# A hybrid block on one core: the first norm taken tile by tile, and the ternary quantiser's pieces moved within the gated steps

## The chip, the cores and the metric

One core of one Trainium2 chip runs one launch. The metric is the device time of that core in microseconds (us); the kernel before takes 2132.3 us (median of three runs, 2129.67 to 2132.58).

## The reference, cut to what matters

x is 2 x 1024 tokens of 512 columns. Four layers are added to it in turn, each on a layernorm of x: a gated linear recurrence ("gated attention"), a feed-forward layer with ternary weights, differential attention, and the same feed-forward layer again. The change lies in the first layer and in the work on the feed-forward weights that is done beside it:

```
proj = layernorm(x) @ w_in.T;  q, k, v, a, g = split(proj, 5)       # 16 heads of 32
q = q * rsqrt(mean(q*q) + eps);  k = tanh(k);  a = clip(sigmoid(a + 2), 0.6, 0.9995)
prefix = cumprod(a) in chunks of 64;  memory = the scan  m = a*m + k*v  over the tokens
y = sigmoid(g) * (q * memory) + (1 - sigmoid(g)) * v;  x = x + y @ w_out.T
# each group of 64 weights of w_gate_up (4096 x 512) and w_proj (512 x 2048):
scale = clip(mean(|w|), 1e-8);  w = scale * clip(round(w / scale), -1, 1)
```

## The kernel before, in words

The kernel has two phases; the change touches only `phase_first` (L265), which holds the gated layer and the first feed-forward layer. The 2048 tokens are four blocks of 512, and a block is four tiles of 128 tokens. The gated layer is 16 **gated steps**, s = 0 to 15; step s works on block s // 4 and on 128 of the 512 output columns (s % 4). The order of work is written out by hand for each engine, and the engines wait for one another on counting semaphores.

In a step TensorE (loop at L467) makes five projections of 128 columns by 512 tokens (`project`, L412, matmuls of L435), in the order q, k, v, a, g. Between them it puts in three one-matmul group sums for the quantiser (`group`, L440, matmul L444), the sums of squares of q (L453) and their spreading by transposes (L460). The three group sums stand after q, after v and after g. I call them **A, B and C** here: A after the first projection of a step, B after the third, C at the end.

The quantiser turns 48 pieces of 128 x 512 weights into ternary form, three in each step. ScalarE makes |w| and sign (`piece`, L538) and issues the load of the piece after next. TensorE's group sum adds |w| over 64 rows. VectorE's `quantise` (L722) reads that sum: L727 writes the scale and increments `scaled`, L730 compares |w| with it and increments `hits`. `hits` releases GpSimd (L647 to L664), which does four bf16 `tensor_tensor` operations on the piece in a row, each waiting for the one before. The group sum of the next piece waits for `scaled` (L443), because it writes the bank that L727 reads.

VectorE's step (L754) is: `finish` of the step before (L738, L740, L743, L749: four operations that end in yT), in some steps the rows of a norm, the first piece, mean and reciprocal for q (L764, L768), the product k*v (L774), the second piece, then a wait for the sigmoid of a (and, where a norm is turned, for its four transposed tiles), the clip (L787, L788), the first scan (L791), L793, the product with q that increments `q_scaled` (L796), the second scan (L798), a copy (L800), the third piece (L807), and in some steps the statistics of a norm. The steps are:

- `STATS_IN`: the statistics of a norm (`normal_stats`, L683: L691, L694, L696) at the end of steps 0, 1, 4, 5, 8, 12.
- `TURN_IN`: two steps later, in steps 2, 3, 6, 7, 10 and 14, the rows of that norm (`normal_rows`, L701: the reciprocal L705, then four `tensor_scalar` operations L708, one for each tile, issued with no wait between them). TensorE transposes rows 0 and 1 after B (`turn`, L388, transposes L397), rows 2 and 3 after the spreading; ScalarE copies each out of PSUM (`keep`, L552). The two PSUM banks are used in turn: tile 2 waits until tile 0 has been taken, tile 3 until tile 1 has. In steps 2, 3 and 7 the norm is of the kind "in" and `keep` frees the bank; in steps 6, 10 and 14 it is of the kind "mid" and VectorE's `keep_low` (L711, L715), which follows ScalarE's copy, frees it.
- `OUT_IN`: in steps 4, 8 and 12 the output projection of a block (L408).

ScalarE's step (L565) has after the copy of v: a wait for VectorE's reciprocal of q (L768), its square root (L586), which releases the spreading; a table load (L589); the two `keep` copies of a turned norm (L555); the sigmoid of a (L594); the third piece.

Before step 0 stands the norm of block 0: VectorE waits for the four tiles of x as they land, does the four statistics, then one variance operation (L696); ScalarE one square root (L550); VectorE the four rows (L708); TensorE transposes (L397), ScalarE copies (L555), and the first projection starts when the fourth copy is done. ScalarE issues the loads of the first two weight pieces (L558, L559) ahead of all that.

Of the kernel before, what the change touches and what calls it, by code (L numbers as in the profile page):

```python
# [9 lines left out]
ALU = mybir.AluOpType  # L10
# [10 lines left out]
TPB = BLK // P  # L21
# [13 lines left out]
class Steps:  # L35
# [5 lines left out]
    def did(self, ins):  # L41
        ins.then_inc(self.sem, 1)
        self.k += 1
        return ins
# [4 lines left out]
    def settle(self):  # L49

        self.eng.wait_ge(self.sem, self.value())
# [5 lines left out]
NP = 3  # L57
# [207 lines left out]
def phase_first(nc, core, x_in, w_inT, w_outT, w_guT, w_pT, wq1, wq2, wk):  # L265

    with ExitStack() as ctx:  # L267
# [41 lines left out]
        vec, gp = sem("s_vec"), sem("s_gp")  # L309
        bank, x = core["banks"], core["x"]  # L310
        W, h16 = core["W"], core["hT16"]
        w_stored = sem("w_stored")
        block = ctx.enter_context(nc.Block())

        def ring(s, j):
# [26 lines left out]
        def x_tile(blk, t):  # L342
            return x[:, (blk * TPB + t) * D:(blk * TPB + t + 1) * D]
# [184 lines left out]
        def _(act):  # L528
            def load(n):
                s, j = divmod(n, NP)  # L530
                i, c = divmod(s, KT)
                if j < 2:
                    src = w_guT[i * P:(i + 1) * P, (2 * c + j) * D:(2 * c + j + 1) * D]
                else:
                    src = w_pT[(i * KT + c) * P:(i * KT + c + 1) * P, :]
                act.dma_start(stage[n % 2], src).then_inc(piece_loaded[n % 2], 16)
# [9 lines left out]
                    load(n + 2)  # L546

            def root(g):
                act.wait_ge(var_ready, g + 1)
                act.activation(dev[g % 2][:, :], var[g % 2][:, :], ACT.Sqrt).then_inc(root_ready, 1)  # L550

            def keep(g, t):  # L552
                kind, blk = of(g)
                act.wait_ge(turned, g * TPB + t + 1)
                act.activation(half(blk, 0, t) if kind == "mid" else whole(blk, t), turn_bank(g, t),  # L555
                               ACT.Copy).then_inc(kept, 1)

            load(0)  # L558
            load(1)  # L559
            root(0)  # L560
            act.preload_act_table_set("sigmoid_and_others")
            for t in range(TPB):
                keep(0, t)
            act.wait_ge(const_ready, 1)
            for s in range(NSTEP):  # L565
                piece(NP * s)
# [100 lines left out]
        def _(dve):  # L667
# [15 lines left out]
            def normal_stats(g):  # L683
                kind, blk = of(g)
                b = g % 2
                for t in range(TPB):
                    if g == 0:
                        dve.wait_ge(first_loaded[t], 16)
                    elif kind == "in" and t == 0:
                        dve.wait_ge(x_loaded[blk], 16)  # L690
                    did(dve.bn_stats(stats[b][:, 6 * t:6 * t + 6], x_tile(blk, t)))  # L691
                settle()
                for t in range(TPB):
                    did(dve.bn_aggr(mv[b][:, 2 * t:2 * t + 2], stats[b][:, 6 * t:6 * t + 6]))  # L694
                settle()
                did(dve.tensor_scalar(var[b][:, :], mv[b][:, 1:2 * TPB:2], LN_EPS,  # L696
                                      1.0 / (UP * UP) if kind == "mid" else 1.0, ALU.add, ALU.mult))
                settle()
                dve.sem_inc(var_ready, 1)

            def normal_rows(g):  # L701
                _, blk = of(g)
                b = g % 2
                dve.wait_ge(root_ready, g + 1)
                did(dve.reciprocal(inv[b][:, :], dev[b][:, :]))  # L705
                settle()
                for t in range(TPB):
                    dve.tensor_scalar(row_of(g, t), x_tile(blk, t), mv[b][:, 2 * t:2 * t + 1], inv[b][:, t:t + 1],  # L708
                                      ALU.subtract, ALU.mult).then_inc(rows_ready, 1)
# [39 lines left out]
                dve.tensor_tensor(yT[:, c * BLK:(c + 1) * BLK], t1[:, :], vc, ALU.add).then_inc(y_ready, 1)  # L749
                dve.wait_ge(y_ready, s + 1)  # L750

            normal_stats(0)
            normal_rows(0)
            for s in range(NSTEP):  # L754
                i, c = divmod(s, KT)
                if s:
                    finish(s - 1)
                g = TURN_IN.get(s)
                if g is not None:
                    normal_rows(g)  # L760
                quantise(NP * s)

                dve.wait_ge(sq_summed, s + 1)
                did(dve.tensor_scalar(mean[:, :], bank[4][:, 0:HPQ], 1.0 / HD, RMS_EPS, ALU.mult, ALU.add))  # L764
                settle()
                if s:
                    dve.wait_ge(spread_root, s)
                dve.reciprocal(inv_q[:, :], mean[:, :]).then_inc(inv_ready, 1)  # L768
                if g is not None:
                    dve.wait_ge(turned, g * TPB + 1)  # L770

                dve.wait_ge(tanhed, s + 1)
                dve.wait_ge(v_kept, s + 1)
                did(dve.scalar_tensor_tensor(t1[:, :], ring(s, 1), 1.0 / FLOOR, v_sb[s % 2], ALU.mult, ALU.mult))  # L774
                settle()
                dve.sem_inc(dve_took, 1)
                quantise(NP * s + 1)
                if s in OUT_IN:
                    for t in (0, 1):
                        add_out(OUT_IN[s], t)  # L780
                if g is not None:
                    for t in (0, 1):
                        keep_low(g, t)
                    dve.wait_ge(turned, g * TPB + TPB)

                dve.wait_ge(sigmoided, s + 1)
                did(dve.tensor_scalar(a_first[:, 0:BLK:CH], ring(s, 3)[:, 0:BLK:CH], 0.6, 0.9995, ALU.max, ALU.min))  # L787
                did(dve.tensor_scalar(a_sb[:, :], ring(s, 3), 0.6, 0.9995, ALU.max, ALU.min))  # L788
                settle()
                dve.sem_inc(dve_took, 1)  # L790
                did(dve.tensor_tensor_scan(prefix[:, :], a_sb[:, :], a_first[:, :], 0.0, ALU.mult, ALU.max))  # L791
                settle()
                did(dve.scalar_tensor_tensor(t1[:, :], prefix[:, :], FLOOR, t1[:, :], ALU.min, ALU.mult))  # L793
                settle()
                dve.wait_ge(spread_done, s + 1)
                dve.tensor_tensor(prefix[:, :], bank[4], q_sb[:, :], ALU.mult).then_inc(q_scaled, 1)  # L796
                start = carry[:, c:c + 1] if i % (NBLK // NB) else 0.0
                did(dve.tensor_tensor_scan(t2[:, :], a_sb[:, :], t1[:, :], start, ALU.mult, ALU.add))  # L798
                settle()
                did(dve.tensor_copy(carry[:, c:c + 1], t2[:, BLK - 1:BLK]))  # L800
                if s in OUT_IN:
                    for t in (2, 3):
                        add_out(OUT_IN[s], t)
                if g is not None:
                    for t in (2, 3):
                        keep_low(g, t)
                quantise(NP * s + 2)  # L807
                if s in STATS_IN:
                    normal_stats(STATS_IN[s])
            finish(NSTEP - 1)  # L810

# [1023 lines left out]
```

## Time and profile before

| what | value |
|---|---|
| median of three runs | 2132.3 us |
| the profiled execution, its own time | 2131.86 us |
| its span, first to last instruction | 2130.0 us |
| PE, DVE, ACT, POOL busy | 96%, 60%, 40%, 42% of the span |
| mean granted TensorE clock, in parts of full speed | 0.989 |
| the 16 gated steps | 14.7 to 398.8 us of the span |

PE is TensorE's matrix unit, DVE is VectorE, ACT is ScalarE, POOL is GpSimd. In a timeline a row gives the start in the span, the duration, the engine, line, operation, what it writes and reads, how many operations were merged (x2), and in brackets how long the engine had been idle before it and what released it.

### The profile page before, as it was taken

The numbers are of one execution on the slowest core, as the hardware profiler recorded it, in microseconds if no ns is written. First come the engines' busy times: TensorE is split into PE (matmuls) and PEld (weight loads), VectorE is DVE, ScalarE is ACT, GpSimd is POOL, SyncE is SP. The second block draws the span as 40 slices with busy tenths as digits, with TensorE's granted clock in tenths as the row PEclk, the third lists the DMA queues.
The fourth block names the chain that finished last, engine by engine and source line by source line (L and its number), as shares of the span: only waits on it lengthen the run. The fifth ranks groups of instructions, "written<-read, shape, count | busy, mean of one in ns | idle before, by whom it ended". The sixth has DMA issues, their size and how long they took to land.

```text
span 2130.0 us, 29410 instructions
## 1 busy us (share of the span) xinstructions
PE 2035.2 (96%) x11824; PEld 902.1 (42%) x11824; DVE 1271.8 (60%) x1838; ACT 855.3 (40%) x1304; POOL 888.4 (42%) x457
## 2 busy tenths in 40 slices
PE   7998999999999999999999999999999879899999
PEld 3444444444444445343434334343433323444444
DVE  5868687647746634455555555555556623775634
ACT  4434353334434322434443434344344442443431
POOL 3766585600000001666666666766766681000000
PEclk9999999999999999999999999999999999999999
DMA  7111110300000011000001010000000101000001
GB/s 232 35 30 35 30 36 30 129 15 1 1 1 1 1 48 26 1 16 14 18 11 21 5 27 1 16 16 16 2 11 6 61 30 40 1 1 20 21 1 40
DMA packets 68999, 55.53 MB, mean 26 GB/s; under 512 B 36800, under 2 KB 55232, under 8 KB 68608
## 3 DMA queue, kind: packets, MB, share of 16 engines
q1 hardware_dynamic: 61952, 41.07, 6.6%
q10 hardware_dynamic: 6912, 12.59, 2.0%
q8 instruction: 94, 1.54, 0.3%
q14 instruction: 41, 0.34, 0.1%
HBM read 43.02 MB, written 10.62 MB: 25 GB/s over the span
## 4 chain that ended last, share of the span: by engine, by line
PE 53%; DVE 4%; ACT 3%; POOL 3%; issue 1%; DVEq 0%; ACTq 0%; POOLq 0%
PE psum L116 9%; PE psum L1151 8%; PE psum L1239 8%; PE psum L1300 6%; PE psum L1283 5%; PE psum L140 5%; PE psum L1189 3%; POOL b_totals L1524 2%; PE psum L1279 2%; PE psum L1245 2%; PE psum L1257 2%; DVE b_maxima L1587 2%; PE psum L1270 1%; PE psum L1197 1%; ACT b_probs L1446 1%
## 5 line engine op out<-in xcount | busy, mean ns | idle before, releaser
L1524 POOL TENSOR_TENSOR b_totals<-b_totals,b_probs 128x2048 f32<-128x2048 f32 (+3 forms) x160 | 515.4, 3221 | 311.1 <-ACT b_probs L1446 304.9
L1587 DVE TENSOR_REDUCE b_maxima<-psum 128x2 f32<-128x1024 f32 (+3 forms) x384 | 350.6, 954 | 392.4 <-PE psum L1245 232.9
L1446 ACT ACTIVATE b_probs<-psum 128x1024 f32<-128x1024 f32 (+3 forms) x320 | 228.6, 765 | 256.4 <-PE psum L1283 233.1
L435 PE MATMUL psum<-hT,a_win 128*128 128x512 f32 x640 | 293.1, 601 | 0.8 <-ACT hT L555 0.8
L116 PE MATMUL psum<-hT,b_early 128*128 128x512 f16 x1024 | 228.2, 383 | 5.2 <-DVE b_middle L202 5.2
L116 PE MATMUL psum<-hT,W 128*128 128x512 f16 x1024 | 226.4, 381 | 3.9 <-DVE a_win L202 3.9
L435 PEld LDWEIGHTS psum<-hT,a_win 128*128 128x128 f32 x640 | 120.4, 193 | 130.8 <-issue 129.5
L116 PEld LDWEIGHTS psum<-hT,b_early 128*128 128x128 bf16 x1024 | 100.2, 98 | 131.5 <-issue 10.6
L116 PEld LDWEIGHTS psum<-hT,W 128*128 128x128 bf16 x1024 | 100.4, 98 | 126.5 <-DVE a_win L202 7.6
L1501 POOL MEMSET b_mask<- 128x128 f32 x1 | 0.2, 204 | 356.8 <-POOLq L267 356.8
L1634 DVE RECIPROCAL b_down<-b_down 128x128 f32<-128x128 f32 x128 | 111.9, 918 | 40.7 <-ACT b_down L1424 40.7
L654 POOL TENSOR_TENSOR a_parts<-a_parts 128x512 bf16<-128x512 bf16 x48 | 60.0, 1251 | 135.2 <-DVE a_parts L730 135.2
L1239 PE MATMUL psum<-b_early 32*128 32x512 f32 (+3 forms) x768 | 106.8, 537 | 6.7 <-ACT b_probs L1446 3.1
L1239 PE MATMUL psum<-b_middle 32*128 32x512 f32 (+3 forms) x768 | 104.9, 538 | 3.9 <-ACT b_probs L1446 2.5
L1446 ACT ACTIVATE b_totals<-psum 128x1024 f32<-128x1024 f32 x64 | 62.0, 1021 | 115.4 <-PE psum L1283 115.4
L202 DVE SCALAR_TENSOR_TENSOR a_win<-psum,a_win 128x512 f32<-128x512 f32 x64 | 44.1, 691 | 99.7 <-ACT a_win L156 98.6
L202 DVE SCALAR_TENSOR_TENSOR b_middle<-psum,lent 128x512 f32<-128x512 f32 x64 | 44.2, 691 | 95.4 <-ACT lent L156 94.8
L156 ACT ACTIVATE lent<-psum 128x512 f32<-128x512 f32 x64 | 38.2, 597 | 150.0 <-PE psum L116 150.0
L1151 PE MATMUL psum<-hT,b_middle 128*128 128x512 f32 x192 | 98.0, 619 | 0.0
L140 PE MATMUL psum<-W,a_parts 128*128 128x512 bf16 x256 | 97.1, 379 | 0.0
L140 PE MATMUL psum<-b_down,b_totals 128*128 128x512 bf16 x256 | 97.1, 379 | 0.0
L140 PE MATMUL psum<-b_down,b_probs 128*128 128x512 bf16 x256 | 97.1, 379 | 0.0
(225 smaller groups left out, 3285.0 us busy)
## 6 DMA issues: line engine op xcount, KB each, us to landing
a_parts<-in_w_guT ACTq DMA_DIRECT2D x32, 256.0 KB, 2.8
ternary<-W SPq DMA_DIRECT2D x1, 6144.0 KB, 18.1
a_win<-in_w_inT SPq DMA_DIRECT2D x20, 256.0 KB, 7.2
a_parts<-in_w_pT ACTq DMA_DIRECT2D x16, 256.0 KB, 2.6
b_down<-lam_rows SPq DMA_DIRECT2D x32, 128.0 KB, 2.7
b_early<-ternary SPq DMA_DIRECT2D x8, 512.0 KB, 7.8
out<-x SPq DMA_DIRECT2D x16, 256.0 KB, 2.2
x<-in_x SPq DMA_DIRECT2D x3, 1024.0 KB, 7.3
```

Source lines behind the costliest of these rows:

```text
L116: last = pe.matmul(self.bank[m % 2 * 2 + part], self.gu[:, k * 2 * HID + col:k * 2 * HID + col + P], self.hT[:, at:at + BLK], start=(k + h ...
L140: last = pe.matmul(self.down_bank(j, t), src[:, m * BLK + t * P:m * BLK + (t + 1) * P], self.wd[:, m * D:(m + 1) * D], start=(m + half == ...
L202: dve.scalar_tensor_tensor(self.h[:, m * BLK:(m + 1) * BLK], self.bank[m % 2 * 2 + 1], 1.0 / UP, self.sg[m % 2], ALU.mult, ALU.mult).then_ ...
L435: last = pe.matmul(ring(s, j), win[:, at:at + P], core["hT"][:, (i * KT + k) * BLK:(i * KT + k + 1) * BLK], start=(k == 0), stop=(k == KT ...
L1151: return pe.matmul(to, weights[:, k * P:(k + 1) * P], hT[:, at:at + BLK], start=(k == 0), stop=(k == KT - 1))
L1239: last = pe.matmul(to[j // 2][:, j % 2, 0:width], strip(qT[w][r % 2], j, qt * P, (qt + 1) * P), strip(kT[w][r % 2], j, kc * BLK, hi), star ...
L1283: last = pe.matmul(to[a][:, j % 2, off:BLK], strip(kT[w][r % 2], j, kt * P, (kt + 1) * P), strip(qT[w][r % 2], j, c * BLK + off, (c + 1) * ...
L1300: last = pe.matmul(bank[6][HEAD_AT[j] * HD:(HEAD_AT[j] + 1) * HD, off:BLK], v_rows[r // 2 % 2][:, at:at + HD], held(u, s)[:, j, off:BLK], ...
L1446: act.activation(held(u, s)[:, 2 * a:2 * a + 2, off:BLK], pair_banks(("score", u, s, a))[:, :, off:BLK], ACT.Exp, scale=SCALE).then_inc(ex ...
L1524: pool.tensor_tensor(acc, acc, held(u, s)[:, :, off:BLK], ALU.add).then_inc(summed, 1)
L1587: dve.tensor_reduce(maxima[u % 2][:, :].rearrange("p (h q c) -> p h q c", h=HPT, q=QT)[:, 2 * a:2 * a + 2, qt, kc], pair_banks(("row", u, ...
L1634: last = dve.reciprocal(rden[k % 2][:, cols], rden[k % 2][:, cols])
```

## The change

Four edits, all in `phase_first`.

1. The norm of block 0 is made tile by tile. VectorE does statistics, aggregation and variance of tile t, then the row of tile t-1; ScalarE takes the square root of one column for each tile, and copies tile t-1 after the square root of tile t. The loads of the first two weight pieces are issued after the square roots of tiles 0 and 1 instead of first, and the table load for the sigmoids comes after the fourth copy instead of before the first.
2. In every step `quantise(NP * s)`, the first piece, stands in front of `normal_rows(g)`; only steps 2, 3, 6, 7, 10 and 14 have rows, so only they change.
3. In steps with neither an output projection nor a turned norm (0, 1, 5, 9, 11, 13 and 15) the third piece is quantised behind L793, in front of L796 and the second scan L798. In the others it stays.
4. Counts of semaphores follow. A wait for `out_added` is set before the statistics in steps that have both; the additions that it waits for are VectorE's own, issued earlier in the same step.

```
@@ ACT
             def root(g):
-                act.wait_ge(var_ready, g + 1)
+                act.wait_ge(var_ready, g)
...
-            load(0)
-            load(1)
-            root(0)
+            def first_root_of(t):
+                act.wait_ge(first_var, t + 1)
+                act.activation(dev[0][:, t:t + 1], var[0][:, t:t + 1], ACT.Sqrt).then_inc(first_root, 1)
+
+            for t in range(2):
+                first_root_of(t)
+                load(t)
+            keep(0, 0)
+            for t in range(2, TPB):
+                first_root_of(t)
+                keep(0, t - 1)
+            keep(0, TPB - 1)
             act.preload_act_table_set("sigmoid_and_others")
-            for t in range(TPB):
-                keep(0, t)
@@ DVE
             def normal_rows(g):
...
-                dve.wait_ge(root_ready, g + 1)
+                dve.wait_ge(root_ready, g)
...
-            normal_stats(0)
-            normal_rows(0)
+            def first_stats(t):
+                dve.wait_ge(first_loaded[t], 16)
+                did(dve.bn_stats(stats[0][:, 6 * t:6 * t + 6], x_tile(0, t)))
+                settle()
+                did(dve.bn_aggr(mv[0][:, 2 * t:2 * t + 2], stats[0][:, 6 * t:6 * t + 6]))
+                settle()
+                dve.tensor_scalar(var[0][:, t:t + 1], mv[0][:, 2 * t + 1:2 * t + 2], LN_EPS, 1.0,
+                                  ALU.add, ALU.mult).then_inc(first_var, 1)
+
+            def first_row(t):
+                dve.wait_ge(first_root, t + 1)
+                did(dve.reciprocal(inv[0][:, t:t + 1], dev[0][:, t:t + 1]))
+                settle()
+                dve.tensor_scalar(row_of(0, t), x_tile(0, t), mv[0][:, 2 * t:2 * t + 1], inv[0][:, t:t + 1],
+                                  ALU.subtract, ALU.mult).then_inc(rows_ready, 1)
+
+            first_stats(0)
+            for t in range(1, TPB):
+                first_stats(t)
+                first_row(t - 1)
+            first_row(TPB - 1)
             for s in range(NSTEP):
...
                 g = TURN_IN.get(s)
+                quantise(NP * s)
                 if g is not None:
                     normal_rows(g)
-                quantise(NP * s)
...
                 did(dve.scalar_tensor_tensor(t1[:, :], prefix[:, :], FLOOR, t1[:, :], ALU.min, ALU.mult))
                 settle()
+                busy = s in OUT_IN or g is not None
+                if not busy:
+                    quantise(NP * s + 2)
                 dve.wait_ge(spread_done, s + 1)
                 dve.tensor_tensor(prefix[:, :], bank[4], q_sb[:, :], ALU.mult).then_inc(q_scaled, 1)
...
-                quantise(NP * s + 2)
+                if busy:
+                    quantise(NP * s + 2)
                 if s in STATS_IN:
+                    if s in OUT_IN:
+                        dve.wait_ge(out_added, (OUT_IN[s] + 1) * TPB)
                     normal_stats(STATS_IN[s])
```

## Rows read from the trace of the kernel before

**Rows 1.** Waits of PE, 0 to 520 us: line waited for, total us, times, longest

```profile
PE psum L444 <- DVE a_parts L727: 19.1, 15, 3.5
```

**Rows 2.** Timeline of PE in steps 1, 2, 3 and 6

```profile
40.75 0.38 PE L444 MATMUL psum<-a_parts,groupones 128*128 128x512 bf16 x1 [0.89 <-DVE a_parts L727]
...
72.95 0.38 PE L444 MATMUL psum<-a_parts,groupones 128*128 128x512 bf16 x1 [3.50 <-DVE a_parts L727]
...
74.07 5.26 PE L435 MATMUL psum<-hT,a_win 128*128 128x512 f32 x8
...
80.48 3.60 PE L435 MATMUL psum<-hT,a_win 128*128 128x512 f32 x8
...
102.86 3.60 PE L435 MATMUL psum<-hT,a_win 128*128 128x512 f32 x8
...
180.32 3.60 PE L435 MATMUL psum<-hT,a_win 128*128 128x512 f32 x8
```

**Rows 3.** Timeline of VectorE in step 2

```profile
70.07 0.18 DVE L705 RECIPROCAL a_inv<-a_dev 128x4 f32<-128x4 f32 x1
70.29 1.00 DVE L708 TENSOR_SCALAR a_t<-x,a_mv,a_inv 128x512 f32<-128x512 f32 x2
...
72.12 0.68 DVE L727 TENSOR_SCALAR a_parts<-psum 128x512 bf16<-128x512 f32 x1
72.83 0.69 DVE L730 SCALAR_TENSOR_TENSOR a_parts<-a_parts 128x512 bf16<-128x512 bf16 x1
```

**Rows 4.** Timeline of VectorE in steps 3 and 6

```profile
93.87 1.50 DVE L708 TENSOR_SCALAR a_t<-x,a_mv,a_inv 128x512 f32<-128x512 f32 x2
...
171.61 0.18 DVE L705 RECIPROCAL a_inv<-a_dev 128x4 f32<-128x4 f32 x1
...
178.04 1.29 DVE L715 TENSOR_TENSOR hT<-psum,hT 128x512 f16<-128x512 f32 x2
```

**Rows 5.** Timeline of GpSimd in steps 2 and 3

```profile
73.61 1.15 POOL L654 TENSOR_TENSOR a_parts<-a_parts 128x512 bf16<-128x512 bf16 x1 [5.57 <-DVE a_parts L730]
...
93.15 1.48 POOL L664 TENSOR_TENSOR W<-a_parts 128x512 bf16<-128x512 bf16 x1
```

**Rows 6.** Timeline of GpSimd, then of VectorE, late in the kernel

```profile
1683.16 4.51 POOL L1524 TENSOR_TENSOR b_totals<-b_totals,b_probs 128x2048 f32<-128x2048 f32 x1 [6.65 <-ACT b_probs L1446]
1687.63 1.45 POOL L1541 TENSOR_TENSOR b_down<-b_down 128x512 f32<-128x512 f32 x1
1689.16 1.26 POOL L1543 TENSOR_TENSOR b_down<-b_down 128x512 f32<-128x512 f32 x1
...
1684.01 3.95 DVE L1670 TENSOR_SCALAR b_early_rows<-x,b_e_mv,b_e_inv 128x512 f32<-128x512 f32 x1
...
1689.08 1.62 DVE L1670 TENSOR_SCALAR b_early_rows<-x,b_e_mv,b_e_inv 128x512 f32<-128x512 f32 x1
```

**Rows 7.** Timeline of ScalarE in step 2

```profile
73.93 0.63 ACT L586 ACTIVATE a_qq<-a_inv_q 128x512 f32<-128x512 f32 x1 [2.25 <-DVE a_inv_q L768]
...
75.87 1.09 ACT L555 ACTIVATE hT<-psum 128x512 f32<-128x512 f32 x2
```

**Rows 8.** Windows: us, PE, PEld, DVE, ACT, POOL busy, PEclk, DMA share, GB/s

```profile
60.00:80.00 20.00, 16.37 (x53) 8.17 (x52) 15.76 (x29) 8.43 (x14) 13.80 (x12) 0.91 0.09 26
```

**Rows 9.** Timeline of VectorE in step 1

```profile
45.20 1.61 DVE L738 TENSOR_TENSOR a_t<-a_prefix,a_t 128x512 f32<-128x512 f32 x1
46.84 0.69 DVE L740 TENSOR_TENSOR a_t<-a_t,lent 128x512 f32<-128x512 f32 x1
```

**Rows 10.** Timeline of VectorE, ScalarE and PE before step 0

```profile
6.95 1.42 DVE L691 BATCH_NORM_STATS2 a_stats<-x 128x6 f32<-128x512 f32 x2 [0.35 <-DMA x<-in_x]
...
9.53 1.91 DVE L708 TENSOR_SCALAR a_yo<-x,a_mv,a_inv 128x512 f32<-128x512 f32 x4
...
14.00 0.60 ACT L555 ACTIVATE hT<-psum 128x512 f32<-128x512 f32 x1 [0.26 <-PE psum L397]
...
14.74 5.97 PE L435 MATMUL psum<-hT,a_win 128*128 128x512 f32 x8 [0.78 <-ACT hT L555]
```

More of the change, by code:

```diff
@@ L311, in phase_first @@
         W, h16 = core["W"], core["hT16"]
-        w_stored = sem("w_stored")
+        w_stored, first_var, first_root = sem("w_stored"), sem("first_var"), sem("first_root")
         block = ctx.enter_context(nc.Block())
@@ L686, in normal_stats @@
                 for t in range(TPB):
-                    if g == 0:
-                        dve.wait_ge(first_loaded[t], 16)
-                    elif kind == "in" and t == 0:
+                    if kind == "in" and t == 0:
                         dve.wait_ge(x_loaded[blk], 16)
```

## The prediction

> **What bounds the kernel now.** I read first the waits of PE over the first 520 us, since the edited code ends at 399 us. PE is busy nearly throughout; what it loses in the gated steps is one kind of wait, 15 times and 19.1 us in all, for L727 of VectorE [rows 1]. The timeline shows where: at group sum A, which waits for the third piece of the step before (0.89 us in step 1), and at group sum B, which waits for the first piece of its own step (3.50 us in step 2) [rows 2]. So VectorE's order sets these waits. The naive sum would promise most of 19.1 us. It isn't to be had: the same VectorE instructions still stand between the sigmoid of one step and the rows that TensorE needs in the next, and PE meets that chain again at the next group sum or at the transposes. Only what leaves or shortens this chain counts.
>
> I write R for the moment at which `normal_rows` starts in a step now (L705: 70.07 us in step 2, 171.61 in step 6; in step 3 93.66, which is 0.21 before the row at 93.87) [rows 3, 4].
>
> **Edit 2, first piece ahead of the rows** (steps 2, 3, 6, 7, 10, 14). Now the reciprocal and four rows take 2.05 us, then L727 and L730 1.4 us [rows 3]. 0.09 us after L730 ends, GpSimd starts its four operations (73.61 against 73.52) [rows 3, 5]. In the new order the rows come just then. What do rows and GpSimd do to each other? In step 3 two rows took 1.50 us instead of 1.00, and ended 0.74 us after a GpSimd operation that ended at 94.63: the row had waited for it [rows 3 to 5]. Later in the kernel the same operation takes 3.95 us under a GpSimd operation and ends 0.29 us after it; another starts 0.08 us before a GpSimd operation, still loses to it, and ends 0.28 us after it, at 1690.70 [rows 6]. And GpSimd's next operation (1687.63), issued before its predecessor had ended, let the waiting row in first and took 1.45 us against 1.26 of its like, 0.19 more [rows 6]. So I take them to alternate: a row, a GpSimd operation, a row.
>
> The new chain then: L727 at R, L730 ends at R+1.40, GpSimd starts at R+1.49. Reciprocal and row 0 would start at R+1.54, so GpSimd is first. Its operation takes 1.15 us [rows 5], to R+2.64; row 0 ends at R+2.93. The others follow at 1.15 + 0.08 + 0.19 = 1.42 us each: R+4.35, 5.77, 7.19. Alone the four take 1.83 us.
>
> On PE: tiles 0 and 1 are transposed after rows 0 and 1, with 0.14 us of handing over (14.60 to 14.74 [rows 10]); tile 1 is done at about R+4.94, projection a (3.43 us in the stream) at R+8.4. On ScalarE: mean and reciprocal of q follow row 3, now 0.41 us from L730's end to L586's start, so L586 starts at R+7.6. It takes 0.63, the table load follows, and the copies start 1.94 after L586 (75.87 - 73.93), at R+9.54; the first ends at R+10.14, the second at R+10.63 [rows 7]. PE's tile 2 waits for the first copy, tile 3 for the second, so projection g starts at R+11.2. Now it starts at R+9.2 in step 3 (102.86 - 93.66) and R+10.4 in step 2 (80.48 - 70.07) [rows 2 to 4]. In the "mid" steps VectorE's two L715 stand behind each copy (0.69, the pair 1.29 [rows 4]): R+12.05, against R+8.7 now in step 6 (180.32 - 171.61) [rows 2, 4]. Steps 7, 10 and 14 repeat 9.2. Sum: 0.8 + 2 x 2.0 + 3.35 + 2 x 2.85 = **13.8 us lost**. L787 waits for these transposes, so the delay is handed to the next step's chain. The second piece's GpSimd work ends earlier relative to L787 than now, so the scan and L793 meet less of it. One such meeting costs 0.92 us (1.61 against 0.69) [rows 9]; I take back **2 us** over six steps, bounds 0 and 5.5 (one meeting per step).
>
> The trace shows no run of rows against a queue of GpSimd. Its bounds: nothing blocked (a gain of some 7 us, below) and 13.8 us. I take the alternation, as every row of rows 6 fits it. The Trainium skill speaks to this and against the change: "SBUF — State Buffer", section "Who interferes with whom", says that VectorE operations in a two-port mode and GpSimd take a shared pair of ports whole, and that issue order decides who blocks. By it each GpSimd operation, issued while a row runs, precedes the next row. The rows agree as far as they go (0.29 us behind the end).
>
> **Edit 3, third piece earlier** (steps 0, 1, 5, 9, 11, 13, 15). VectorE runs the same instructions, so the chain keeps its length, apart from meetings with GpSimd, and the A waits that vanish (0.89 in step 1) reappear at B. The group sum C is done by then. q_scaled comes 1.4 us later, still before the next q is projected. GpSimd's work moves about 2.6 us earlier, so its meetings move from L738 and the variance of the statistics to the second scan. In steps 0 and 5 statistics follow, which lose nothing to GpSimd, and L738 is then free: -0.8 and -1.0. In 9 and 13 +0.2 each; 1 and 11 nothing; behind step 15 one meeting more delays the feed-forward layer that follows, +0.85. Each is one or two times the 0.92 us of a meeting [rows 9]. Sum **-0.7**, bounds -3 and +3 (three meetings).
>
> **Edit 1, first norm.** Now the last tile's statistics end at 8.37, the rows start at 9.53, the last copy starts at 14.00, projection q at 14.74 [rows 10]. Pairs of transposes and copies take turns on two banks, about 1.1 us from a tile's first transpose to its copy. Statistics, aggregation and variance of a tile alone take some 1.1 us, reciprocal and row 0.7. With tiles landing as now (the third tile's statistics at 6.95), the square root of tile 3, queued behind the copy of tile 1, gives row 3 at 12.4 and projection q at 14.45: 0.3 gained. But half a megabyte of weight pieces no longer shares the DMA engines with x. If the tiles land 1 to 1.7 us sooner, q starts at 13.2. I take **-1.2**; bounds +0.5 and -3 (with an earlier rise of the clock: the 8 matmuls from 14.74 take 5.97 us against 3.60 later [rows 2, 10]). The pieces are needed only after that and their loads stay hidden; if they were late, group sum A of step 0 would wait 1 or 2 us.
>
> **Clock.** In step 2 the idle 3.50 us was followed by matmuls at the lower level (5.26 us against 3.60; 0.91 granted in that stretch) [rows 2, 8]: 1.66 us. The new order has longer stretches with little PE work, from B to tile 1, but much of it lies under ScalarE's chain. +0.5, bounds -2 and +4.
>
> **Sum** against the profiled execution's own 2131.9 us (span 2130.0, 1.9 around it; the median is 0.4 higher): 13.8 - 2 - 0.7 - 1.2 + 0.5 = +10.4, so 2142.3; against the median **2142.5 us**.
>
> **Rivals.** (a) *GpSimd blocks row 0 only, the others follow in a burst.* For it: rows are issued 0.46 us apart with no semaphore between; against it: the GpSimd operation of 1687.63, likewise issued without a gap, which the waiting side overtook [rows 6]. Rows end at R+4.3, projection g starts at R+8.7 ("in") or R+9.15 ("mid"): -1.7 in step 2, -0.5 in 3 and 7, +0.4 in 6, 0 in 10 and 14, in all -2.3. With -0.7 and -1.2, 2128.1. (b) *Rows and GpSimd don't meet at all, VectorE faster.* Row 0 is at R+2.1; tile 0 starts 0.85 us sooner in steps 2 and 6, 1.3 in the others: -6.9, the lower clock of step 2 gone, -1.7: 2122. Against it stand rows 4 to 6. This is the other side; it decides if a row after L730 wins the ports, 0.05 us being the margin. (c) *Alternation, but the later waits overlap more than I think* (all 5.5 us of meetings saved, -3 at the start with an early rise of the clock, no fall of it in step 2, -2): 13.8 - 5.5 - 0.7 - 3 - 2 = +2.6, 2134.5.
>
> **How the numbers follow.** Alternation at its price 0.70, (c) 0.12, (a) 0.11, (b) 0.07. The alternation's own bounds give 2137 to 2149. With (c) and (a) the range is 2128 to 2149, leaving out (b) and one in ten of the rest. What a measurement of this kernel can tell from no change is 0.2%, 4.3 us: slower means over 2136.6, faster under 2128.0. Slower 0.69; same 0.18 (most of (c) and half of (a)); faster 0.13.
>
> **What would show it.** Right: in the turned steps L708 as separate rows of about 1.4 us, ending some 0.3 us after GpSimd operations that grew to about 1.35; PE waiting at L397 for L708 and ScalarE's or VectorE's copies, where it waited at L444; A waits left only in steps 7, 11, 15; L738 short in step 1; projection q of step 0 near 13.5. Wrong: rows at 0.46 us spacing behind one blocked row (a), or none blocked (b); projection g under R+9.5; the waits of L444 gone with nothing in their place.

## The result, and the profile after

| | before | after |
|---|---|---|
| median of six runs each, us | 2131.05 | 2143.68 |
| lowest to highest, us | 2129.67 to 2132.58 | 2143.44 to 2145.75 |
| ratio of after to before, 95% interval | | 1.0058 [1.0048, 1.0069] |
| span of the profiled execution, us | 2130.0 | 2141.6 |

The changed kernel is 12.6 us slower, 1.2 us from the forecast, and outside what a measurement could confuse with no change. First the waits of PE in the first 530 us of the kernel after (line waited for, total us, times, longest). Lines of VectorE have moved: L732 and L735 are the two operations of `quantise`, L710 and L713 the reciprocal and the rows.

```profile
PE psum L397 <- DVE a_t L713: 12.4, 12, 1.9
...
PE psum L444 <- DVE a_parts L732: 6.7, 8, 1.7
PE psum L116 <- DVE a_win L202: 4.8, 2, 4.3
...
PE psum L397 <- ACT hT L555: 2.5, 3, 0.9
PE psum L397 <- DVE hT L720: 1.0, 2, 0.7
```

The wait at L444 fell from 19.1 us to 6.7 [rows 1]. In its place stand waits of the transposes L397 for the rows (12.4 us, two in each of the six turned steps), for ScalarE's copies (2.5 us, of which 0.6 lies before step 0 and 0.94 each in steps 3 and 7) and for VectorE's (1.0). Next the timeline of VectorE in step 2 (start, us, engine, line, operation, tiles, count, and in brackets the idle time before; compare [rows 3]). R, the start of `quantise`, is 66.63.

```profile
66.63 0.69 DVE L732 TENSOR_SCALAR a_parts<-psum 128x512 bf16<-128x512 f32 x1
67.35 0.69 DVE L735 SCALAR_TENSOR_TENSOR a_parts<-a_parts 128x512 bf16<-128x512 bf16 x1
...
68.17 2.68 DVE L713 TENSOR_SCALAR a_t<-x,a_mv,a_inv 128x512 f32<-128x512 f32 x2
70.77 1.37 DVE L713 TENSOR_SCALAR a_prefix<-x,a_mv,a_inv 128x512 f32<-128x512 f32 x1
72.06 1.37 DVE L713 TENSOR_SCALAR a_a<-x,a_mv,a_inv 128x512 f32<-128x512 f32 x1
```

That of GpSimd in the same step (compare [rows 5]):

```profile
68.12 1.15 POOL L661 TENSOR_TENSOR a_parts<-a_parts 128x512 bf16<-128x512 bf16 x1 [3.53 <-DVE a_parts L735]
69.35 1.21 POOL L663 TENSOR_TENSOR a_parts<-a_parts 128x512 bf16<-128x512 bf16 x1
70.64 1.21 POOL L665 TENSOR_TENSOR a_parts<-a_parts 128x512 bf16<-128x512 bf16 x1
71.93 1.22 POOL L671 TENSOR_TENSOR W<-a_parts 128x512 bf16<-128x512 bf16 x1
```

And that of PE in steps 2 and 3 (compare [rows 2]):

```profile
67.47 0.38 PE L444 MATMUL psum<-a_parts,groupones 128*128 128x512 bf16 x1 [1.73 <-DVE a_parts L732]
69.70 0.63 PE L397 MATMUL psum<-ident,a_t 128*128 128x128 f32 x4 [1.86 <-DVE a_t L713]
70.99 1.08 PE L397 MATMUL psum<-ident,a_t 128*128 128x128 f32 x4 [0.66 <-DVE a_t L713]
71.87 4.85 PE L435 MATMUL psum<-hT,a_win 128*128 128x512 f32 x8
...
77.86 3.60 PE L435 MATMUL psum<-hT,a_win 128*128 128x512 f32 x8
...
100.88 0.65 PE L397 MATMUL psum<-ident,a_prefix 128*128 128x128 f32 x4 [0.94 <-ACT hT L555]
...
101.86 3.60 PE L435 MATMUL psum<-hT,a_win 128*128 128x512 f32 x8
```

The group sum B comes early, but the four rows take 5.26 us (68.17 to 73.43) instead of 1.91 (70.29 to 72.20 [rows 3]), and GpSimd's four operations lie between them. Row 0 ends at 69.55, 0.28 us after the first of them. PE waits 1.86 us for row 0 and 0.66 us for row 1 and starts projection g at 77.86 = R+11.23. In step 3 it starts at 101.86 (R+10.90; R is 90.96 there), behind a wait of 0.94 us for ScalarE's copy. In step 2 no such wait stands ahead of g: the eight matmuls of projection a take 4.85 us there, not 3.60, and PE itself arrives late. The start of the kernel, in PE's timeline (compare [rows 10]):

```profile
12.51 5.58 PE L435 MATMUL psum<-hT,a_win 128*128 128x512 f32 x8 [0.78 <-ACT hT L555]
```

Projection q starts 2.23 us sooner than at 14.74, and its eight matmuls take 5.58 us, as before not at full pace.

Where the time went is read best from one mark in each step, ScalarE's sigmoid of g (L602 before; L609 after). The table gives its start before, and for each kernel below how much later (+) or sooner (-) its mark comes; the last line is the first L202 of the feed-forward layer. "first piece", "third piece" and "first norm" are the edits alone.

| step | before | after | first piece | third piece | first norm | GpSimd waits | rows between |
|---|---|---|---|---|---|---|---|
| 0 | 36.25 | -2.63 | +0.17 | -2.22 | -1.09 | -2.90 | -2.36 |
| 1 | 57.57 | -3.42 | +0.17 | -3.01 | -1.08 | -3.68 | -3.14 |
| 2 | 84.11 | -2.61 | +0.77 | -3.46 | -2.77 | -6.21 | -6.26 |
| 3 | 106.50 | -1.01 | +2.62 | -3.84 | -3.17 | -7.04 | -7.57 |
| 5 | 158.53 | -1.01 | +2.62 | -3.84 | -3.18 | -6.49 | -7.58 |
| 6 | 183.95 | +0.95 | +5.82 | -4.80 | -1.47 | -6.79 | -9.07 |
| 7 | 207.11 | +2.65 | +7.33 | -4.80 | -1.02 | -7.43 | -10.06 |
| 9 | 259.14 | +2.64 | +7.33 | -4.81 | -1.03 | -6.88 | -9.73 |
| 10 | 282.70 | +5.35 | +9.86 | -5.01 | -0.95 | -7.47 | -10.48 |
| 12 | 336.02 | +4.97 | +9.80 | -5.31 | -0.94 | -7.42 | -10.47 |
| 14 | 378.71 | +8.64 | +12.35 | -5.48 | -0.93 | -8.01 | -11.21 |
| 15 | 398.83 | +8.15 | +12.35 | -5.50 | -0.94 | -7.65 | -10.92 |
| L202 | 408.50 | +9.07 | +12.36 | -4.57 | -0.93 | -6.73 | -9.99 |

### The profile page after: what moved, and what is told of

Same layout as the page of the kernel before. It is cut to its first block, busy times and chain, and to the rows that moved or that the text cites. A ratio compares the mean times of both kernels' runs of the same rounds, so it can differ in the third digit from the quotient of the medians.

```text
span 2141.6 us, 29406 instructions
## 1 busy us (share of the span) xinstructions
PE 2045.0 (95%) x11824; PEld 905.7 (42%) x11824; DVE 1287.7 (60%) x1844; ACT 855.3 (40%) x1307; POOL 883.5 (41%) x457
## 4 chain that ended last, share of the span: by engine, by line
PE 53%; DVE 4%; ACT 3%; POOL 3%; issue 1%; DVEq 0%; ACTq 0%; POOLq 0%
PE psum L116 9%; PE psum L1181 8%; PE psum L1269 8%; PE psum L1330 6%; PE psum L1313 5%; PE psum L140 5%; PE psum L1219 3%; POOL b_totals L1554 2%; PE psum L1309 2%; PE psum L1275 2%; PE psum L1287 2%; DVE b_maxima L1617 2%; PE psum L1300 1%; PE psum L1227 1%; ACT b_probs L1476 1%
## 5 line engine op out<-in xcount | busy, mean ns | idle before, releaser
L435 PE MATMUL psum<-hT,a_win 128*128 128x512 f32 x640 | 296.4, 607 | 0.8 <-ACT hT L555 0.8
L435 PEld LDWEIGHTS psum<-hT,a_win 128*128 128x128 f32 x640 | 122.0, 195 | 134.8 <-issue 133.5
L202 DVE SCALAR_TENSOR_TENSOR a_win<-psum,a_win 128x512 f32<-128x512 f32 x64 | 44.1, 691 | 100.1 <-ACT a_win L156 98.7
L202 DVE SCALAR_TENSOR_TENSOR b_middle<-psum,lent 128x512 f32<-128x512 f32 x64 | 44.2, 691 | 95.3 <-ACT lent L156 94.8
L156 ACT ACTIVATE lent<-psum 128x512 f32<-128x512 f32 x64 | 38.2, 597 | 150.0 <-PE psum L116 150.0
L140 PE MATMUL psum<-W,a_yo 128*128 128x512 bf16 x256 | 97.0, 379 | 0.0
```

What stands on the lines that cost most here:

```text
L140: last = pe.matmul(self.down_bank(j, t), src[:, m * BLK + t * P:m * BLK + (t + 1) * P], self.wd[:, m * D:(m + 1) * D], start=(m + half == ...
L202: dve.scalar_tensor_tensor(self.h[:, m * BLK:(m + 1) * BLK], self.bank[m % 2 * 2 + 1], 1.0 / UP, self.sg[m % 2], ALU.mult, ALU.mult).then_ ...
L435: last = pe.matmul(ring(s, j), win[:, at:at + P], core["hT"][:, (i * KT + k) * BLK:(i * KT + k + 1) * BLK], start=(k == 0), stop=(k == KT ...
```

## The experiments

The verdict of each is against the kernel before on the same chip. Runs 1 to 3 do one edit alone.

**1. The first piece alone (edit 2).**

```
+                quantise(NP * s)
                 if g is not None:
                     normal_rows(g)
-                quantise(NP * s)
```

> The kernel before with edit 2 alone: the first piece quantised ahead of the rows in the six turned steps. Theory (each row waits for a GpSimd operation that hit released, rows and GpSimd alternate): L708 rows end about 1.3 us apart, the six turned steps cost together some 12 to 14 us, time 2143 to 2147. Rival 1 (the loss of the whole change comes from the third piece or the first norm, edit 2 gives what its order promises): 2124 to 2131. Rival 2 (only row 0 is blocked, the loss lies in the lower TensorE clock): rows after the first 0.46 us apart, 2130 to 2137.

Measured: 2144.08 against 2132.18 us, ratio 1.0057 [1.0042, 1.0072]. The rows of step 2 in this kernel (VectorE's timeline; here they are L708, as before):

```profile
71.79 2.68 DVE L708 TENSOR_SCALAR a_t<-x,a_mv,a_inv 128x512 f32<-128x512 f32 x2
74.40 1.37 DVE L708 TENSOR_SCALAR a_prefix<-x,a_mv,a_inv 128x512 f32<-128x512 f32 x1
75.69 1.37 DVE L708 TENSOR_SCALAR a_a<-x,a_mv,a_inv 128x512 f32<-128x512 f32 x1
```

The rows end 1.29 us apart: alternation, and rival 2 (a burst behind one blocked row) falls. The table shows the whole loss in the six turned steps (2, 3, 6, 7, 10, 14): +0.60, +1.85, +3.20, +1.51, +2.53, +2.55, together 12.2 us. Edit 2 alone is as slow as the whole change, so rival 1 falls too.

**2. The third piece alone (edit 3).**

```
+                busy = s in OUT_IN or g is not None
+                if not busy:
+                    quantise(NP * s + 2)
                 dve.wait_ge(spread_done, s + 1)
...
-                quantise(NP * s + 2)
+                if busy:
+                    quantise(NP * s + 2)
```

> The kernel before with edit 3 alone: third piece ahead of the second scan in steps 0, 1, 5, 9, 11, 13, 15. Theory (the chain of VectorE keeps its length, vanished waits at group sum A reappear at B; only meetings with GpSimd move): -0.8 us in step 1, -1.0 in step 6, 0 in steps 10 and 14, about 0.9 us more ahead of the feed-forward layer; 2130 to 2133 in all. Rival (the A waits of 4.7 us in all are simply gone): 2127 to 2128, with no B wait grown.

Measured: 2132.69 against 2132.18 us, 1.0007 [0.9997, 1.0018]. Its waits of PE:

```profile
PE psum L444 <- DVE a_parts L727: 17.5, 10, 3.8
```

and in its timeline of PE the group sums B of steps 1 and 10 and the wait ahead of the feed-forward layer:

```profile
46.84 0.38 PE L444 MATMUL psum<-a_parts,groupones 128*128 128x512 bf16 x1 [1.22 <-DVE a_parts L727]
...
268.23 0.38 PE L444 MATMUL psum<-a_parts,groupones 128*128 128x512 bf16 x1 [2.31 <-DVE a_parts L727]
...
404.68 5.73 PE L116 MATMUL psum<-hT,W 128*128 128x512 f16 x13 [4.26 <-DVE a_win L202]
```

Five waits at A have gone, and the sum at L444 fell only from 19.1 to 17.5 us: they came back at B (1.22 us in step 1 instead of 0.89 + 0.97; 2.31 in step 10 instead of 1.20 + 1.14). Steps 1 and 6 gained 0.79 and 0.96 us, as forecast; ahead of the feed-forward layer 0.93 us was added. Steps 2 and 3 gained 0.45 and 0.38 us that weren't forecast. The rival falls. The -2.2 us at step 0, where this kernel is the same as before up to the mark, comes from the pace of the first matmuls (last section).

From step 0 to L202 the trace gained 2.35 us in all, and the median none. Part of it goes in the first microseconds of the feed-forward layer: ScalarE's first L156, at 414.21 us before, comes only 3.02 us sooner here, where L202 came 4.57 sooner. The windows of 14 us from some 4 us ahead of L202, of before and of this run (columns as in [rows 8]; the granted clock is the last but two), are

```profile
404.00:418.00 14.00, 10.66 (x43) 4.56 (x42) 7.40 (x8) 2.68 (x5) 5.25 (x4) 0.88 0.56 169
```

```profile
400.00:414.00 14.00, 9.74 (x32) 3.61 (x31) 6.83 (x8) 2.34 (x4) 3.19 (x3) 0.76 0.67 214
```

Behind the longer wait more of the layer's start ran at the lower level (0.76 granted, not 0.88). In runs 4 and 10 the same window reads 0.76 too, and they lose 1.56 and 1.50 us from L202 to L156. It isn't the longer wait alone: run 5 and the kernel after have the longest wait there too (4.3 us), with 0.88 granted, and lose 0.4 us.

**3. The first norm alone (edit 1).** The kernel after with edits 2 and 3 undone.

> The kernel before with edit 1 alone: the norm of block 0 tile by tile. Theory: the first group sum comes 2.6 us sooner, as in the kernel after (17.92 against 20.55), and nothing later gives it back: 2128 to 2130. Rival (the steps absorb it, or the clock's rise moves): 2131 to 2133.

Measured: 2131.44 against 2132.18 us, 0.9997 [0.9987, 1.0006]: no difference that can be told. Projection q of step 0 starts 1.7 us sooner (13.02 against 14.74), the end of step 0 comes 1.09 us sooner, and 0.93 us of it is left at the feed-forward layer. Between them the marks swing: its step 2 has no stretch at the lower level, where the kernel before has one (granted clock 0.86 from 72 to 84 us), and gains 1.7 us; its step 6 has one (0.88 from 170 to 184, before 1.00) and loses 1.7. Whether the 0.93 us survive to the end the run can't tell; the time is one that the rival gave, and a gain of the size expected isn't there.

**4. GpSimd waits for the rows.** The kernel after, plus:

```
                 pool.wait_ge(w_sign, n + 1)
+                if j == 0 and s in TURN_IN:
+                    pool.wait_ge(rows_ready, (TURN_IN[s] + 1) * TPB)
```

> The kernel after, in which GpSimd waits for the four rows before it starts the first piece of a turned step; nothing is left out. Theory (the rows are slow because of GpSimd and of nothing else): rows 0.46 us apart as before the change, projection g of a turned step at R + 7.9 to 8.4 instead of 10.9 to 12 (R: start of the first piece), no drop of the clock around 375 us, time 2120 to 2127. Rival (the rows are slow for their place behind L735, or the loss is in ScalarE's chain or the clock): unchanged rows or 2138 to 2144.

Measured: 2128.67 against 2132.18 us, 0.9985 [0.9975, 0.9994], 15 us less than the kernel after, a little above the range given. Step 2 in VectorE's timeline (rows are L715, the first piece L734 and L737, R = 66.36), then in PE's:

```profile
67.09 0.69 DVE L737 SCALAR_TENSOR_TENSOR a_parts<-a_parts 128x512 bf16<-128x512 bf16 x1
...
67.90 1.00 DVE L715 TENSOR_SCALAR a_t<-x,a_mv,a_inv 128x512 f32<-128x512 f32 x2
68.82 0.54 DVE L715 TENSOR_SCALAR a_prefix<-x,a_mv,a_inv 128x512 f32<-128x512 f32 x1
69.28 0.54 DVE L715 TENSOR_SCALAR a_a<-x,a_mv,a_inv 128x512 f32<-128x512 f32 x1
```

```profile
68.60 1.08 PE L397 MATMUL psum<-ident,a_t 128*128 128x128 f32 x8 [1.02 <-DVE a_t L715]
...
74.26 3.60 PE L435 MATMUL psum<-hT,a_win 128*128 128x512 f32 x8
```

The same rows in the same place take 1.92 us, projection g starts at R+7.90. Nothing else was changed, so the rows are slow because of GpSimd's operations beside them, and not because of their place. This is the run that settles the cause.

**5 and 6. The cut: scale, rows, comparison.** Since B waits for the scale alone, and GpSimd starts on the comparison alone, the rows can stand between them:

```
-            def quantise(n):
+            def quantise(n, between=None):
...
                 dve.tensor_scalar(sc[b], bank[5], ...).then_inc(scaled, 1)
+                if between is not None:
+                    between()
                 dve.wait_ge(scaled, n + 1)
...
-                quantise(NP * s)
-                if g is not None:
-                    normal_rows(g)
+                quantise(NP * s, None if g is None else lambda: normal_rows(g))
```

> The kernel after, with the piece of a turned step cut in two: L727 (scale, which frees group sum B), then the four rows, then the comparison that releases GpSimd. Theory (what harms is hit ahead of the rows, the early scale is good): rows 0.46 us apart, tile 0 some 0.7 us sooner than in the run where GpSimd waits for the rows, in the four steps where PE waited 1.02 us for it; 2124 to 2128. Rival (the wait moves on to ScalarE's chain, nothing gained over that run's 2128.7): 2128 to 2131.

Measured: 2123.34 (2123.05 to 2124.34) against 2132.36 us, 0.9958 [0.9944, 0.9972]. It beats both kernels: 20 us under the kernel after. Step 2 (R = 66.90) in VectorE's timeline, in PE's, and the waits of PE:

```profile
66.90 0.69 DVE L732 TENSOR_SCALAR a_parts<-psum 128x512 bf16<-128x512 f32 x1
...
67.72 1.00 DVE L713 TENSOR_SCALAR a_t<-x,a_mv,a_inv 128x512 f32<-128x512 f32 x2
68.64 0.54 DVE L713 TENSOR_SCALAR a_prefix<-x,a_mv,a_inv 128x512 f32<-128x512 f32 x1
69.09 0.54 DVE L713 TENSOR_SCALAR a_a<-x,a_mv,a_inv 128x512 f32<-128x512 f32 x1
69.55 0.68 DVE L737 SCALAR_TENSOR_TENSOR a_parts<-a_parts 128x512 bf16<-128x512 bf16 x1
```

```profile
68.41 1.08 PE L397 MATMUL psum<-ident,a_t 128*128 128x128 f32 x8 [2.39 <-DVE a_t L713]
...
74.21 3.60 PE L435 MATMUL psum<-hT,a_win 128*128 128x512 f32 x8
```

```profile
PE psum L444 <- DVE a_parts L732: 5.5, 7, 1.4
...
PE psum L397 <- DVE a_t L713: 3.3, 4, 2.4
```

In step 2 row 0 ends at R+1.4 and tile 0 starts at R+1.5, where it started at R+3.1 both before and after. The rival falls: the gain is 5 us over run 4. Then the same with the third piece moved in steps 0 and 5 only (`busy = s not in (0, 5)`):

> The same, with the third piece moved only in steps 0 and 5, where the run of edit 3 alone gained 0.79 and 0.97 us; in step 15 that edit added 0.92 us to the wait ahead of the feed-forward layer. Theory: that wait is back at 3.34 us, 0.9 us less than in the run before this, and with one stretch of lower clock behind it instead of two; 2122 to 2127. Rival (steps 10 and 14 lose with the old order what step 15 gives back): no difference between the two.

Measured: 2126.32 (2122.73 to 2126.86) against 2132.36 us, 0.9967 [0.9954, 0.9979], not told apart from run 5. The wait ahead of the feed-forward layer did fall back, but its L202 came 1.25 us later than in run 5 (-8.74 against -9.99): steps 11 and 15 lost 1.00 and 1.02 us against step 10 and step 14, where run 5 lost 0.3 in each. So far the rival was right. But at the start of the feed-forward layer the theory was: the granted clock is 1.00 from 396 to 410 us, against 0.88 from 395 to 409 in run 5, and by the first L156 this kernel is 10.03 us ahead of before, run 5 only 9.61. The times don't decide between the two.

**7. q ahead of the rows.** The kernel after with `normal_rows(g)` behind the reciprocal of q instead of ahead of it.

> The kernel after, with mean and reciprocal of q (L788, L792) ahead of the four rows of a turned step, so that ScalarE's root, table load and copies no longer wait for row 3. Theory (rows alternate with GpSimd still; part of the loss goes through ScalarE's chain): rows still 1.3 us apart, PE's waits for ScalarE's and VectorE's copies at tiles 2 and 3 gone, projection g at R + 9.5 to 10 instead of 10.9 to 12.5; about 1 us less in each turned step, 2135 to 2140. Rival (the loss is all in tiles 0 and 1): unchanged 2142 to 2145.

Measured: 2141.15 against 2132.36 us, 1.0041 [1.0027, 1.0054]. The waits of PE:

```profile
PE psum L397 <- DVE a_t L713: 13.9, 12, 4.0
...
PE psum L397 <- DVE hT L720: 0.8, 1, 0.8
...
PE psum L397 <- ACT hT L555: 0.6, 1, 0.6
```

The waits for ScalarE's copies fell from 2.5 to 0.6 us, and the 0.6 is the one before step 0: in the turned steps none is left. Those for rows rose from 12.4 to 13.9 (longest 4.0: row 0 is later). Projection g of step 3, in PE's timeline (R is 91.71 there):

```profile
101.40 3.60 PE L435 MATMUL psum<-hT,a_win 128*128 128x512 f32 x8
```

In steps 3 and 7 it starts at R+9.69, as the theory had it, against R+10.90 in the kernel after. In steps 2, 6 and 10 projection a ran at the lower level (5.27, 5.37 and 5.30 us instead of 3.60), and g starts only at R+11.66, 11.76 and 11.27. So a share of the loss went through ScalarE's chain, some 1.2 us in each of steps 3 and 7. The time, 2141.15, lies in neither range, 1.15 above the theory's and 0.85 below the rival's, and its interval overlaps that of the kernel after, so the time doesn't show the share.

**8 and 9. What gains at the start.** Edit 1 alone, but `load(0)` and `load(1)` ahead of everything as before:

> Edit 1 alone, but with the loads of the first two weight pieces issued first, as before the change. Theory (half of the gain at the start is that x no longer shares the DMA engines with these loads): the first statistics at 4.4 to 4.5 us as before instead of 3.3, projection q of step 0 at 14.0 to 14.6 instead of 13.0. Rival (the gain is in the tile by tile order alone): projection q at 13.0 to 13.2.

and the kernel before with only these loads moved behind `root(0)`:

> The kernel before with one change: the loads of the first two weight pieces are issued after the square root of the first norm instead of ahead of it; the norm keeps its old order. With the loads first, the tile by tile order brought projection q of step 0 only to 14.53 us, against 14.74 before and 12.5 to 13.0 with both. Theory now (the gain at the start is the DMA engines left to x, hardly the order): the four tiles land by 6.0 to 6.3 us instead of 6.9, the rows start near 8.0 to 8.7 instead of 9.53, projection q at 13.0 to 13.9. Rival (it takes both): projection q at 14.4 or later.

Measured, one run of each: 2132.57 against 2132.36, and 2128.8 against 2129.98 us. The first projection in PE's timeline of the run of the tiles, then of that of the loads, and the first statistics of the latter in VectorE's:

```profile
14.53 5.85 PE L435 MATMUL psum<-hT,a_win 128*128 128x512 f32 x7 [0.78 <-ACT hT L555]
```

```profile
13.65 3.67 PE L435 MATMUL psum<-hT,a_win 128*128 128x512 f32 x8 [0.78 <-ACT hT L555]
```

```profile
3.47 1.32 DVE L691 BATCH_NORM_STATS2 a_stats<-x 128x6 f32<-128x512 f32 x2 [1.03 <-DMA x<-in_x]
```

Tile by tile alone brings 0.2 us, the loads alone 1.1 us, both together 1.7 to 2.2 (13.02 and 12.51). The first tile's wait for its load is 1.03 us there, and its statistics start at 3.47, where the kernel after has 3.41. So the greater part is the loads moved out of the way of x, and the order of the norm gains little without that. The times of single runs decide nothing here; the starts of projection q do.

**10. Edits 1 and 3 without 2.**

> The kernel after with edit 2 undone: first norm tile by tile and third pieces early, rows again ahead of the first piece. Theory (the whole loss of the change is edit 2, the other two together are worth about what they gained alone, a little under 3 us): 2129 to 2132, and no row that waits for GpSimd beyond those of the kernel before. Rival (edits 1 and 3 work against each other, or hide a loss of their own): over 2133.

Measured: 2132.69 against 2132.48 us, 0.9997 [0.9988, 1.0007]. The time lies between the ranges of theory and rival. No loss hides in them, and no gain that can be measured either, although the mark at step 15 stood 4.66 us sooner and L202 3.74. Some 1.5 us of that is lost at the start of the feed-forward layer, as in run 2.

**11. The cut alone,** on the kernel before.

> The kernel before with nothing but the cut of the first piece of a turned step: L727, then the four rows, then the comparison. Theory (this cut is what gave rows_between its gain; the turned steps 2, 3, 6, 7, 10, 14 together 6 to 7 us shorter than before at the end of step 15, start unchanged): 2124 to 2128. Rival (rows_between owes its gain to edits 1 and 3): 2129 to 2132.

Measured: 2125.91 (2122.75 to 2128.48) against 2132.48 us, 0.9962 [0.9949, 0.9974]. Its mark at step 15 is 4.45 us sooner, less than the 6 to 7 expected: step 6 gained 0.56 instead of 1.5, and steps 11 and 15 lost 1 us each, both for want of the early third pieces: run 6, which has them in steps 0 and 5 alone, gained 1.5 us in step 6 and lost the same 1 us in 11 and 15. The cut gives 6.6 us where run 5 gives 9.0, and the intervals overlap.

## Why the prediction was right, and where it was off

- **What bounds the steps.** "PE meets that chain again" held: in run 2 waits moved from A to B and the time stayed. The 19.1 us were never there to be had.
- **Alternation of rows and GpSimd.** Right; it was argued from rows late in the kernel, and shown by runs 1, 4 and 5. The size was a little off: 1.29 us a row, not 1.42, since GpSimd's operations grew to 1.21 us, not to 1.34. The Trainium skill ("SBUF — State Buffer", "Who interferes with whom") says that a VectorE operation in a two-port mode and a GpSimd operation exclude each other from the shared ports for the whole instruction, and that issue order decides who blocks. The rows agree in that each kind holds the other up: 0.46 us from row to row without GpSimd at work (run 4), 1.29 with it. "Whole" can't be read as the recorded time, though: 1.15 + 0.46 = 1.61 us, and a pair takes 1.29. That it is the ports no run shows by itself; that it is GpSimd, run 4 does.
- **Price per turned step,** forecast and run 1: 0.8 and 0.6 in step 2, 2.0 and 1.85 in step 3, 3.35 and 3.20 in step 6, 2.0 and 1.51 in step 7, 2.85 and 2.53, 2.55 in steps 10 and 14. Sum 13.85 and 12.2. The 1.6 us between them look like the 2 us that I took back for later meetings, but they aren't. Projection g of run 1 starts at R+10.99, 10.89, 11.90, 10.90, 11.73 and 11.74; before, it starts at R+10.41, 9.20, 8.71, 9.21, 9.21 and 9.21. That is 12.20 us later in sum, the whole price. So the 1.6 us are the closer rows, and of the meetings nothing was saved (in step 2 the scan L791 took 2.03 us, before 1.86, and L793 1.46 and 1.47). Two wrong terms, 13.85 and -2, cancel here but for 0.4 us, which is luck.
- **Projection g at R+11.2:** R+11.23 in step 2, but R+10.90 in step 3 (101.86 - 90.96). The closer match is luck: in step 2 it was the lower clock on projection a that set the start of g, and not the path of my sum through ScalarE's copies. That path is seen in steps 3 and 7, with a wait of 0.94 us for a copy, and g comes 0.3 us sooner than forecast. In the "mid" steps 6 and 10 it is R+11.6, forecast 12.05.
- **Third pieces.** -0.8, -1.0 and +0.85 came as -0.79, -0.96 and +0.93. L738 is short in step 1, as I said (0.69 us in the kernel after, before 1.61). The +0.2 in steps 10 and 14 were -0.2, step 12 gave 0.3, and steps 2 and 3 gave 0.8 together. My own terms add up to -0.55, not to the -0.7 that I wrote; the trace has -2.35 to L202, and then the 1.55 us lost at the start of the feed-forward layer, which no term of mine held. The run's median is 0.5 us above that of before, no more than noise.
- **First norm.** The term -1.2 had the right mechanism and the wrong size in the trace: projection q came at 12.51, not 13.2, because the first tile landed 1.0 us sooner than before, nearer to the early end that I allowed for. The mark of step 0, -2.63, also holds an earlier rise of the clock (last section). In the times the term can't be seen (run 3).
- **Clock.** The term +0.5 is the least founded. Beside step 2, three turned steps of the kernel after had stretches at the lower of the two levels that they hadn't had. The windows of after (stretch and its length, then busy us of PE, PEld, DVE, ACT and POOL, the granted clock, DMA):

```profile
170.00:180.00 10.00, 6.85 (x21) 3.64 (x21) 9.22 (x13) 4.45 (x7) 5.71 (x5) 0.83 0.00 0
270.00:285.00 15.00, 12.00 (x39) 6.25 (x38) 13.37 (x19) 7.21 (x11) 8.89 (x8) 0.89 0.06 18
372.00:384.00 12.00, 9.47 (x30) 5.27 (x31) 9.55 (x14) 6.03 (x9) 8.05 (x7) 0.72 0.00 0
```

  PE had waited 1.9 us for row 0 right before each. In step 14 the change cost 3.67 us (8.64 - 4.97), with edit 2 alone, at full clock there, 2.55: some 1.1 us are the clock's (0.72 granted from 372 to 384). Behind L202 a further 2.5 us were lost (11.6 of span less 9.07), in code that the change doesn't touch, and not in one place: 0.4 up to 414 us of before (the first L156), 0.3 up to 485, 0.4 up to 853, 0.5 up to 1403, and 1.0 behind VectorE's last addition (2135.46 against 2124.81, still 10.65 later), in the storing of the output. That last microsecond isn't TensorE's clock, and run 5, 8 us faster than before, loses it too; the cause of these parts stays open.
- **Rivals.** (b) fell by the rows of L713 in the kernel after, (a) by their spacing, (c) by the sum. (c) had counted on meetings saved, and none were. The sum, +10.4 on 2131.9, met 2143.68 within 1.4 us. The mechanism that carries it was right; the closeness is in part luck, since the trace had +9.07 at L202, 1.3 less than the sum, and the 2.5 us behind L202 were in no term.

## What to carry to other kernels

Ask not only what a moved instruction waits for but what it releases: here the comparison of the first piece, set ahead of the rows, set free 5 us of GpSimd work that took turns with them. The turned steps became 0.6 to 3.2 us longer (run 1), where the same first piece, cut in two, makes them 0.7 to 3.1 us shorter (run 5). A helper that signals twice (bank free, work ready) can be cut between the two signals; run 11 got 6.6 us below the kernel before from that alone, run 5 9.0 with the other edits, and their intervals overlap. And when an engine's chain is the bound, a wait that vanishes at one place of another engine comes back at the next; add up the chain, not the waits.

## What the runs showed of the hardware that I had not expected

The 25 runs of the kernel before beside runs 1 to 4 fall into three groups: ten from 2129.77 to 2130.45, eight from 2132.09 to 2132.54, seven from 2133.91 to 2134.89. Kernels whose code is the same up to there differ by as much at the first group sum of step 0: it starts at 20.55 before, and at 18.34 in run 2. The reason is in the traces. The groups of PE's instructions of L435 (count, busy us, mean ns) of before, from 14 to 19 and from 19.5 to 24 us:

```profile
L435 PE MATMUL psum<-hT,a_win 128*128 128x512 f32 x5 | 4.6, 1087 | 0.8 <-ACT hT L555 0.8
L435 PE MATMUL psum<-hT,a_win 128*128 128x512 f32 x11 | 5.2, 603 | 0.0
```

and of run 2 from 14 to 19 us:

```profile
L435 PE MATMUL psum<-hT,a_win 128*128 128x512 f32 x10 | 4.7, 600 | 0.8 <-ACT hT L555 0.8
```

The first matmuls of before are recorded at 1.06 us (the very first at 1.19), and those from 19.69 us on at 0.59. The trace's records of TensorE's granted clock begin at full level, 2.4 GHz, at 19.37 us in before and at 14.51 us in run 2. In the kernel after they begin at 16.35 us, in run 3 at 18.93, and in runs 8 and 9 at 19.77 and 12.88; in each of these traces the matmuls change from 1.06 to 0.59 us at that moment, or are at 0.59 from the first one where it lies before them. So the slow first matmuls ran at the lower level, 1.2 GHz, and what differs between two executions of the same start is when the clock rose. A window ahead of the first record reads 1.00 (10 to 22 us, in before as in run 2), but only because no lower level is recorded there.

This explains the marks of step 0: projection q of run 3 starts 1.72 us sooner than before and the clock rises only 0.44 us sooner, so the mark gains 1.09; in run 9 the clock was up before the first matmul, and the mark came 3.4 us sooner, more than in any other kernel here. Whether it also makes the three groups of times isn't shown. A difference of 2 us between two executions says nothing, then, and edits worth 1 or 2 us, like 1 and 3, are read from traces by marks that start behind this point, or need many runs.
